# Node rows and edges of a four-layer graph network laid out last first

## What is computed

```python
x = _layernorm(x + L0(x))   # edge MLP on [x[src], x[dst]], times edge_weight, segment_sum over dst
x = _layernorm(x + L1(x))   # two SAGE convolutions: h @ W_self + mean over dst of h[src] @ W_neigh + b
x = _layernorm(x + L2(x))   # two GCN convolutions: segment_sum over dst of h[src] * norm
x = _layernorm(x + L3(x))   # attention: softmax over edges of one source, segment_sum over dst, projection
```

```python
src = jax.random.randint(..., (50000,), 0, 50000)
dst = minimum((50000 * uniform(..., (50000,)) ** 2.0).astype(int32), 49999)
_o = argsort(dst, stable=True); src = src[_o]; dst = dst[_o]
```

## Time and profile before

| what | value |
|---|---|
| median of 3 runs | 7317.93 us (7313.45 to 7320.28) |
| span of the profiled execution | 7317.8 us |
| POOL busy | 4231.4 us, 58% |
| PE busy | 4978.7 us, 68% |
| DVE busy | 4095.9 us, 56% |
| ACT busy | 2782.5 us, 38% |
| agg0 | about 1178 to 1610 us |
| agg1, agg2 | 1893 to 2430, 2429 to 2952 us |
| agg3, agg4 | 3284 to 3824, 4019 to 4549 us |
| agg5 | 6495 to 7060 us |
| mean granted TensorE clock | 0.771 of 2.4 GHz |

### The profile page before, as it was taken

How to read it: one execution, slowest core, us unless ns; L and a number is a source line. 1 busy time by engine, 2 the same in 40 slices (tenths; PEclk the granted TensorE clock), 3 DMA queues, 4 the chain that set the end, 5 groups by cost and what they waited for, 6 DMA issues and landing times. The chain is left out here.

```text
span 7317.8 us, 134052 instructions
## 1 busy us (share of the span) xinstructions
PE 4978.7 (68%) x26557; PEld 3921.4 (54%) x26558; DVE 4095.9 (56%) x13682; ACT 2782.5 (38%) x6869; POOL 4231.4 (58%) x4642
## 2 busy tenths in 40 slices
PE   4666676779666576996679566766666666425677
PEld 3555554558556465774557465544444444315555
DVE  4555557877323123664775123876666666553568
ACT  1555553237224135781343134941111111101259
POOL 3777771005677677007760776457777777537730
PEclk7777778999657558995899568977777777655789
DMA  1222223559546334883558356942222222213468
GB/s 30 75 74 75 74 73 124 185 196 383 180 131 190 89 96 126 302 287 87 152 183 275 91 159 204 301 141 70 70 70 70 69 70 70 60 39 82 110 198 292
DMA packets 560379, 1016.33 MB, mean 139 GB/s; under 512 B 118515, under 2 KB 127121, under 8 KB 559889
## 3 DMA queue, kind: packets, MB, share of 16 engines
q1 hardware_dynamic: 229424, 419.18, 17.7%
q10 hardware_dynamic: 197568, 359.75, 14.2%
q0 software_dynamic: 133280, 236.29, 12.9%
HBM read 624.60 MB, written 390.17 MB: 139 GB/s over the span
## 5 line engine op out<-in xcount | busy, mean ns | idle before, releaser
L448 PE MATMUL agg_bank<-agg_msgs,agg_onehot 128*128 x7840 | 1504.4, 353 | 703.0 <-DVE agg_onehot L386 568.5
L448 PEld LDWEIGHTS agg_bank<-agg_msgs,agg_onehot 128*128 128x128 f32 x7840 | 1299.3, 251 | 976.0 <-issue 970.4
L386 DVE TENSOR_TENSOR agg_onehot<-iota,rel 128x512 f32<-128x512 f32 x1176 | 814.8, 693 | 1421.0 <-SPq L354 727.8
L317 POOL DMA_INDIRECT agg_msgs<-y,agg_rows x784 | 782.4, 998 | 236.8 <-issue 197.1
L483 ACT ACTIVATE agg_kept<-agg_bank,inv_root 128x128 f32<-128x128 f32 x784 | 223.5, 368 | 710.8 <-PE agg_bank L448 691.5
L448 PE MATMUL agg_bank<-agg_weighted,agg_onehot 128*128 x1568 | 342.1, 389 | 219.7 <-DVE agg_onehot L386 167.3
L483 ACT ACTIVATE agg_kept<-agg_bank,inv_deg 128x128 f32<-128x128 f32 x784 | 223.4, 368 | 698.9 <-PE agg_bank L448 680.9
L314 POOL DMA_INDIRECT agg_weight<-weights,agg_rows x392 | 414.8, 1058 | 123.3 <-issue 98.9
L1108 POOL DMA_INDIRECT mlp_xs<-in_x,mlp_rows x392 | 406.8, 1038 | 116.7 <-issue 115.7
L1404 POOL DMA_INDIRECT by_source<-score_line,score_places x392 | 388.9, 992 | 127.2 <-issue 120.1
L317 POOL DMA_INDIRECT agg_msgs<-near,agg_rows x392 | 388.2, 990 | 117.6 <-issue 96.3
(11 more groups left out here) (332 smaller groups left out, 12812.4 us busy)
## 6 DMA issues: line engine op xcount, KB each, us to landing
sums<-agg_kept ACTq DMA_DIRECT2D x490, 256.0 KB
agg_first<-y ACTq DMA_DIRECT2D x196, 256.0 KB
messages<-mlp_m SPq DMA_DIRECT2D x98, 256.0 KB, 2.1
agg_first<-in_x ACTq DMA_DIRECT2D x98, 256.0 KB
agg_msgs<-messages SPq DMA_DIRECT2D x98, 256.0 KB
l_z<-sums SPq DMA_DIRECT2D x98, 256.0 KB
x<-l_o POOLq DMA_DIRECT2D x98, 256.0 KB
near<-l_near_o SPq DMA_DIRECT2D x98, 256.0 KB
```

The lines of the kernel that those rows point to most:

```text
L317: pool.indirect_dma_start(msgs[:, j, :], None, table[:, :], bass.IndirectOffsetOnAxis(ap=rows[:, third, j:j + 1], axis=0)).then_inc(sm[f"g ...
L386: nc.vector.tensor_tensor(onehot[:, j, :, :], k.iota[:, 0:P].unsqueeze(1).to_broadcast([P, Q, P]), k.rel[:, ds(i * (4 * Q) + j * Q, Q)].un ...
L448: t.matmul(bank[:, column[q], :], onehot[:, j, q, :], messages[:, slot[q], :], start=False, stop=True, skip_group_check=True)\
```

## The change

The host turns the order of nodes and edges over (`[::-1]`) and pads at the end as before; the output is turned back. On the chip `setup` computes `N - 1 - node` for all targets and sources, so that tables, staircase and gathers go by the new numbers. The targets are still in ascending order then. No line of `aggregate` or of another stage differs. The padded source is given as a number that turns into the same `PAD_SRC`, and the padded target into the same 60000.

```diff
+def turned_over(node):
+    return N - 1 - node
...
+        from_i, to_i = sb("from_i", [P, ET], I32), sb("to_i", [P, ET], I32)
...
-                c.link(v.tensor_copy(dst_f[:, :], k.dst_i[:, :]))
+                for turned, given in ((to_i, k.dst_i), (from_i, k.src_i)):
+                    c.link(v.tensor_scalar(turned[:, :], given[:, :], -1, N - 1, ALU.mult, ALU.add))
+                c.link(v.tensor_copy(dst_f[:, :], to_i[:, :]))
...
-                for to, node in ((k.dst_row, node_i), (k.src_row, k.src_i)):
+                for to, node in ((k.dst_row, node_i), (k.src_row, from_i)):
...
-                for to_lo, to_hi, node in ((k.src_lo, k.src_hi, k.src_i), (k.dst_lo, k.dst_hi, k.dst_i)):
+                for to_lo, to_hi, node in ((k.src_lo, k.src_hi, from_i), (k.dst_lo, k.dst_hi, to_i)):
...
-    arrays = {"x": by_four(rows(inputs["x"], 0))}
-    arrays["src"] = by_tile(inputs["src"], PAD_SRC)
-    arrays["src_rows"] = rows(inputs["src"], PAD_SRC)[None, :]
-    arrays["dst"] = by_tile(inputs["dst"], PAD_DST)
-    arrays["edge_weight"] = by_tile(inputs["edge_weight"], 0)
+    def last_first(name):
+        return np.asarray(inputs[name])[::-1]
+
+    arrays = {"x": by_four(rows(last_first("x"), 0))}
+    arrays["src"] = by_tile(last_first("src"), turned_over(PAD_SRC))
+    arrays["src_rows"] = rows(last_first("src"), turned_over(PAD_SRC))[None, :]
+    arrays["dst"] = by_tile(last_first("dst"), turned_over(PAD_DST))
+    arrays["edge_weight"] = by_tile(last_first("edge_weight"), 0)
...
-    arrays["mask"] = by_tile(inputs["edge_attr_8"], 0).reshape(P, ET * HEADS)
+    arrays["mask"] = by_tile(last_first("edge_attr_8"), 0).reshape(P, ET * HEADS)
...
-    return r.results[0]["out_0"].reshape(GROUPS, P, Q, C).swapaxes(1, 2).reshape(NP, C)[:N]
+    return r.results[0]["out_0"].reshape(GROUPS, P, Q, C).swapaxes(1, 2).reshape(NP, C)[:N][::-1]
```

## The result

The changed kernel takes **7280.8 us** (median of 4 runs, 7272.8 to 7288.7) against 7319.05 us before. The ratio is 0.9952, with a 95% interval of 0.9936 to 0.9967. That is 38 us faster, where 48 were forecast (7270, range 7252 to 7306). The profiled execution has a span of 7287.1 us, so it stands at the slow end of the runs, and that of the second measurement has 7271.5.

A forecast was written before the change was run, and what follows sets the result against it. POOL's gather issue was taken to bound agg1 to agg5, with the consumers slower late in each stage. Tails 57.6 less new start 5, DVE contention 3.5 and setup 0.8 gave 48 us: 7318 - 48 = 7270 us, range 7252 to 7306.

The forecast's parts named there:

- The tails: Ends of agg1 to agg5: time from last gather to last matmul falls from 90.6 us to 5 x 6.6, saving 57.6.
- The new start: Start of agg1 to agg5: POOL fills the ring ahead of slower steps and waits 1 us a stage, 5 us.
- rival (a): New stage starts: PE stays near its lower clock, POOL waits 9 us a stage, leaving 8 us gain: 7310 us; chance 0.13.
- Rival (b): New stage starts: bank work and PE make four steps cost 2.4 us, so the kernel gets slower: 7372 us; chance 0.07.
- DVE beside POOL: agg1 to agg5: one-hots moved beside gathers lengthen them by 0.09 us each, 0.7 us a stage, 3.5 us in all.
- the sign that I had set: agg1 to agg5: first to last gather stays within 3 us; 8 us or more longer, with early POOL waits, means wrong.
- "some eight": One-hots per stage, agg1 to agg5, that ran after the last gather and would run beside one: 0.7 us a stage.
- The hard reading of the rule: agg1 to agg5: each of eight moved one-hots holds a gather for its whole 0.69 us, 5.5 a stage, 28 in all.
- agg0: Aggregate stage without gathers, bound by step rate: its mix is mirrored, so 0 us, at most 7 us either way.
- Setup: Chain ahead of everything: two added DVE operations of 128 x 392 whole numbers cost 0.8 us, surely under 1.2.
- Other stages: Edge MLP, scores, softmax and dense stages: equal work per group and random sources as before, costed at 0.
- the chance of 0.80: Whole kernel: chance that it is faster, meaning below 7303 us; 0.13 for the same, 0.07 for slower.

The follow-up runs named there:

- the second measurement: The changed kernel run again with no edit: 7273.2 us, ratio 0.9949 to the kernel before.
- run 2: Changed kernel with POOL held to at most 8 to 12 tiles ahead in agg1 to agg4: 7291.6 us, ratio 0.9970 to the kernel before.
- run 3: Kernel before the change, with POOL's lead limited to 8 to 12 tiles: 7315.8 us against 7315.6, ratio 1.0003.
- run 4: Changed kernel with the one-hots' counting row read from PSUM, one SBUF input instead of two: 7222.3 us, ratio 0.9878 to the kernel before.
- run 7: Kernel before, with an unused 768-column DVE comparison ahead of each one-hot (stages without a tally) and the counting row in PSUM: 7259.5 us.
- run 8: Kernel before, with an unused 448-column DVE comparison ahead of each one-hot: 8583.3 us on a chip where the kernel before took 8545.4.
- run 9: Kernel before, with an unused 256-column DVE comparison ahead of each one-hot: 8562.9 us on a chip where the kernel before took 8545.4.
- Run 5: Kernel before the change, with the one-hots' counting row read from PSUM: 7266.5 us, ratio 0.9933.

## Why the prediction was right, and where it was off

**The tails.** Forecast 90.6 - 5 x 6.6 = 57.6 us. Measured 90.6 - 33.3 = 57.3. Taking the new end from the stage's own start was sound: 6.3 to 6.6 us in four stages, 7.6 in agg5. Runs 2 and 3 show the mechanism, not only the size: a shorter lead costs 18 us in the new order and nothing in the old.

**The new start, forecast 5 us.** It cost 0 to 2 us. The gaps between gathers sum to 620.9 us over the five stages before, and to 622.5 and 620.7 in the two profiles of the changed kernel. Its waits of POOL for PE are 0.3 us each in agg1 and agg3 and single ones of up to 2.4 us elsewhere, much as before, so rival (a) did not happen. It was near: with the lead held to 8 to 12 tiles, waits of 1.8 us are there (run 2). PE ran at a granted clock of 0.81 in the first 100 us, not at 0.51. It did 349 matmuls in 100 us that hold some 9 us without any, 1.9 steps a us, the same rate as late in the old order. Rival (b) is gone with that.

**DVE beside POOL, forecast 3.5 us: this term was mis-sized, it is 18 to 21 us.** The way from first to last gather grew by 22.9 us in one profile and 18.2 in the other, against 8.5 for this term and the last one together. By the sign that I had set, within 3 us a stage, it failed in four stages of the first profile and three of the second, and agg4 of the second reached 8.3 us, with no waits of POOL piling up. It is the gathers themselves. In the second profile their means over the five stages are 10, 12, 7, 23 and -6 ns above those of before, 46 in sum, times 392 is 18 us: all of it. I had spread the excess of the earlier trace rows over all one-hots, 0.09 us each. It isn't spread so. These are the gathers of agg1 in five stretches, POOL's busy time and count of L317, kernel before:

```profile
1897.00:1999.00 102.00, 77.07 (x81) 0.50 0.31 86
1999.00:2101.00 102.00, 77.09 (x81) 0.55 0.38 109
2101.00:2203.00 102.00, 77.47 (x78) 0.62 0.50 148
2203.00:2305.00 102.00, 78.25 (x77) 0.75 0.61 187
2305.00:2407.50 102.50, 78.29 (x77) 0.84 0.67 203
```

and of L326, changed kernel:

```profile
1899.00:2003.00 104.00, 80.32 (x76) 0.81 0.68 205
2003.00:2106.00 103.00, 79.40 (x76) 0.90 0.67 201
...
2313.00:2417.00 104.00, 78.61 (x83) 0.51 0.24 65
```

A gather takes 951 ns where the steps wait for it, and 1016 and 1017 where they run freely. In the changed kernel the two free stretches cost 1057 and 1045. While the steps wait, a one-hot starts when a gather has landed, and this falls a little after another gather has started; it costs nothing. Run freely, it may lie over a gather's start. Here is one of each kind, early in the changed agg1:

```profile
1987.07 0.69 DVE L395 TENSOR_TENSOR agg_onehot<-iota,rel 128x512 f32<-128x512 f32 x1 [0.96 <-PE agg_bank L457]
1987.23 1.35 POOL L326 DMA_INDIRECT agg_msgs<-near,agg_rows  x1 [0.31 <-issue]
...
1990.38 0.95 POOL L326 DMA_INDIRECT agg_msgs<-near,agg_rows  x1 [0.30 <-issue]
1990.62 0.69 DVE L395 TENSOR_TENSOR agg_onehot<-iota,rel 128x512 f32<-128x512 f32 x1 [1.37 <-ACT agg_bank L481]
```

Runs 4, 7, 8 and 9 show that the one-hot is the cause and that its moment sets the price. The Trainium skill (GPSIMD Engine Reference, Specifications) names this contention, and run 4 bears it out with 1008 against 945 ns.

Which one-hots cost more can be read from the same traces. These are the ones of agg1 that start after the last gather, before and in the changed kernel:

```profile
L386 DVE TENSOR_TENSOR agg_onehot<-iota,rel x7: 691/692/693, 2407.7 to 2417.4; 128x512 f32<-128x512 f32 x7
```

```profile
L395 DVE TENSOR_TENSOR agg_onehot<-iota,rel x2: 693/693/693, 2416.4 to 2420.1; 128x512 f32<-128x512 f32 x2
```

Over the five stages there were 32 such one-hots before (7, 6, 5, 7, 7), and there are 10 now. Turned over, the same 32 run beside gathers, and these are held by them for 4.3 us in one profile and 2.1 in the other. That is what the 3.5 us were for, and it was right. But the other one-hots, which ran beside gathers in both orders, hold them for 11 and 14 us more than before (85 us before, 96 and 99 after). The rest lies in gathers that start under no one-hot. So the step of the prediction that failed is that only the "some eight" one-hots a stage that move were priced, and the price of all the others was left as it was. The hard reading of the rule, 28 us, came nearer to the measured 18 to 21 than my 3.5, but by chance, since it too prices only the eight.

Why the others cost more is open. It is not that more of them run freely: in agg1 to agg4 295 of 784 wait for SP to pass on that a gather has landed before, and 293 and 294 do in the changed kernel. What changed is where they fall against the starts of the gathers, and no run moved that in the changed kernel alone.

Run 5 limits what follows from this. Take the contention away on both sides and the order is not seen to be worth more than before (40 us). Then POOL fills the ring sooner and waits. So it can't be said that the 18 us could be had back by curing the gathers; the slower side of the new start, the steps, claims it.

**agg0**, forecast 0, at most 7 us: the first matmul of its steps to the last takes 417.6 us before and 415.6 after (1187.0 to 1602.6). **Setup**, forecast 0.8 us: the next stage begins at 94.3 us in both profiles and at 94.9 in the second one of the changed kernel. The two operations take 0.36 us each, as priced. **Other stages**, forecast 0: the edge MLP differs by 3 us in one profile and by less than 0.3 in the other, the score stage by 0.3 and by -6. They gather beside DVE as well, and how their starts fall may be what spreads the runs of one kernel over 16 us. That is argued, not shown.

The result is in the range and within the chance of 0.80 for faster than 7303. The forecast was 11 us too low against the first median and 3 against the second. The main term and its mechanism were right. That the second comes so near is luck in part: the term for DVE beside POOL was 15 us too small, and it was made up by the new start, by 2 us in agg0 and by 6 us in the score stage, of which the last two were costed at 0.

## What to carry to other kernels

When a producer bounds most of a stage and the consumer the rest, the order of the work decides whether the buffer between them is of use: let the consumer-bound part come first, and the stock that builds up is spent; let it come last, and it is a tail. Before turning such an order, work out the lead that it wants and compare it with the buffer. And price contention by what a single instruction costs another one, and for all pairs whose timing the new order shifts, not only for those that newly meet. The part of the old trace where the engines run freely would not have been enough: its 154 gathers at 1016 and 1017 ns are 11 us over 95 one-hots, 0.12 us each. By my estimate from these, eight of them in five stages cost some 5 us, and not 18. An operand moved to PSUM can be worth more than the order.

## What the runs showed of the hardware

- An indirect gather on POOL takes 0.94 us. If it starts while a DVE comparison with two SBUF inputs runs, it takes as much longer as is left of that, less about 0.12 us (0.53, 0.47, 0.26 and 0.19 us left gave 0.41, 0.35, 0.14 and 0.08 more). In agg1, agg2, agg3 and agg4 of the kernel before this holds to within 0.03 us for all 210 gathers that start more than 0.045 us into a one-hot with over 0.16 us of it left. A gather that starts within the first 0.043 us of one is not held, and there the one-hot ends 0.72 us after the gather's start, so it takes up to 0.77 us and not 0.69. If the comparison starts 0.04 us or more inside the gather, neither is longer (0.95 and 0.69 us).
- With one of the two inputs in PSUM the comparison takes the same 0.69 us and no gather is held: mean 945 against 1008 ns. In this kernel that alone is worth 47 to 51 us.
- Together with the turned order it gave the fastest version here, 7222.3 us, ratio 0.9878 to the kernel before.
